# A one-core kernel of two graph layers: row products one unit later in layer 0, and two reload sequences of the second step reordered

## The chip, the cores and the metric

The kernel runs on one core of a Trainium2 chip. The metric is the device time of one execution in microseconds (us). The engines are named as the profile names them: PE (TensorE), DVE (VectorE), ACT (ScalarE), POOL (GpSimd) and SP (SyncE), which issues all DMAs of this kernel in one order.

## The reference

N = 4096 nodes, 256 features. Layer 0 is a dense graph attention layer with 4 heads, layer 1 a two-step diffusion with a learned sparse attention; each is followed by a residual and a layer norm.

```python
# layer 0
h = inputs @ W                                   # hr = h as (N, 64, 4)
e = s_src[:, None, :] + s_dst[None, :, :]        # N x N x 4
e = where(e >= 0, e, -0.2 * e)
att = softmax(e * adj[:, :, None], axis=1)
out = einsum('ijh,jfh->ihf', att, hr) + bias + inputs @ res_w + res_b
x = layernorm(x + out)
# layer 1
R = adj + eye; R = R / R.sum(-1)                 # N x N
for n in range(2):
    A = top_p_attention(Xa, W1, W2, W3)          # softmax(q k^T), nucleus 0.9, rows renormalised
    Xf = R @ Xf
    Xa = A @ Xa
    Z = Z + Xf @ U1[n].T + Xa @ U2[n].T
x = layernorm(x + layernorm(x + Z))
```

## The kernel before, in words

Rows are worked in 32 tiles of 128 (NT = 32). Every engine has its own program, written out by hand, and semaphores tie them together; no scheduler moves anything.

**Layer 0** has 128 units u, one for each tile t = u // 4 and head h = u % 4. DVE makes the masked scores of a unit in `masked(u)`: an addition (L1386), the leaky step (L1388), and the multiplication with the tile's adjacency rows and row maximum (L1390), which waits for the adjacency tile (semaphore `s_adj`). Its result goes through one small POOL instruction (L568), which raises `s_u`; ACT waits for that in `ex(u)` (the exponential, L1063). ACT then does `linear(u + 2)` (L1057), whose result DVE's L1388 of unit u + 2 waits for, and four copies of transposed chunks out of PSUM, `ev` (L1070). PE transposes the chunks (`turn`, L845) and multiplies them with the features (`pv`, L796). Once in a tile there are further pieces. In unit u % 4 = 0 ACT copies the tile's output (`out_turned`, L1104) and a transposed normalised tile (`ev_x`, L1080), and PE does `turn_back` (L804 to L809). In the next unit ACT copies the residual output (`ev_y0`, L1096). In unit u % 4 = 2 and 3 DVE does the layer norm (`post_a`, `post_b`).

The **row products** `rows(r)` on PE (L835, L828) multiply the normalised tile r of the layer's result with the two matrices U1 and the key and query matrix; `ev_rows(r)` on ACT (L1086, L1087) copies them out and raises `s_gx`. SP stores them: it waits for `s_gx`, issues three stores (`xf_d`, `gx_d`, `kq_d`), and then, in the next turn of its loop, loads the next adjacency tile (`in_adj`, 2 MB) into the one of two buffers that came free, stores the normalised tile (`X_d`) and loads a piece of xT:

```python
for t in range(NT + 3):
    if 1 <= t < NT:
        if t >= 2: sp.wait_ge(s_u, 4 * (t - 1))
        ld(adj_s[t % 2], tile_of(adj, t), s_adj[t % 2])
    ...
    if 2 <= t < NGX + 2:
        r = t - 2
        sp.wait_ge(s_gx, 2 * (r + 1))
        ...
```

**Layer 1** keeps the two operands `xa` and `xf` whole in SBUF (32 row tiles each). A step s does for each tile n the logits (`logits`, L927), the search of the nucleus threshold on DVE (L1477 to L1610) with help of POOL (`bracket`, L600 to L623) and ACT (`level`, L1235 and L1236), the transposes (`Tr`, L972), the product with `xa` (`AV`, L986), and the small products (`mq`, L950). In the second step (s = 1) PE also does `Rmul(r)` (L911), 32 matmuls (eight for each of four chunks) of a row tile of adj with `xf`, to which POOL adds the unit matrix's part: r = 0 to 31 is the first hop and r = 32 to 63 the second, whose operand is the first hop's result y. A row tile of R needs four chunks of 512 KB (`adjTb`), which go through three buffers; SP loads chunk q + 3 once PE is through with chunk q (semaphore `R`). PE does Rmul(0) and Rmul(1) ahead of the tile loop, then two of them in each tile, and `gather_level(n)` (L992) between, ahead of which DVE can't finish its tile (L1591 waits for it). POOL's `r_post` normalises a row tile of R's product, SP stores it (`rstore`: `y_d` for the first hop, `z_d` for the second). `xa` is loaded again ahead of the second step (`reload`, from `xa_d`), `xf` is loaded again from `y_d` ahead of Rmul(32) (`chunked(xf, y_d)`), eight loads of four row tiles each (semaphores `s_xl[0..7]`).

Of the kernel before, what the change touches and what calls it, by code (L numbers as in the profile page):

```python
# [26 lines left out]
def gat_topp_kernel(nc, xT, x, adj, adjTb, Wp, WT, aT, res_w, bias, res_b, ident, sel,  # L27
                    W1, W2T, W3T, U1T, U2T, ln_g, ln_b, out):
    N = adj.shape[0]
    NT = N // 128  # L30
    TBK = min(8, NT)
    NCH = NT // TBK
# [10 lines left out]
    AJR = 3  # L43
    XA = 257
    NQ = N // 512
    HT = NT // 2
    CT = 4
# [8 lines left out]
    def pairs_in(n):  # L56
        if n < 0:
            return [0]
        if n == 0:
            return list(range(1, RLEAD + 1))  # L60
        return [n + RLEAD] if n + RLEAD < NT else []

    ctx = ExitStack()
    with ctx:
# [21 lines left out]
        def sem(name):  # L86
            return ctx.enter_context(nc.semaphore(name))
# [30 lines left out]
        ys = cst.take(2, 256)  # L118
# [32 lines left out]
        xf = r1.take(NT, XA)  # L151
# [6 lines left out]
        u2 = r1.take(2, 256)  # L158
# [48 lines left out]
        y_d = nc.dram_tensor("y_d", [N, 256], F32).ap()  # L207
# [14 lines left out]
        def tile_of(d, t):  # L222
            return d[t * 128:(t + 1) * 128, :]
# [62 lines left out]
        s_l1 = sem("s_l1")  # L286
# [16 lines left out]
        gslot = {}  # L303
        i = 0
        for u in range(NU):
            if u % 4 == 1 and u >= 9:
                gslot[(u - 9) // 4] = i
                i += 1
            for c in range(NCH):
                slot_of[u * NCH + c] = i  # L310
                i += 1
            if u % 4 == 0 and u >= 8:
                xslot[(u - 8) // 4] = i
                i += 1
# [7 lines left out]
        st = []  # L322
        for s in range(2):
            g = {}
# [17 lines left out]
        def _(sp):  # L342
            def ld(dst, src, s):
                sp.dma_start(dst, src).then_inc(s, 16)
# [59 lines left out]
            qload(0, 0)  # L404
            qload(0, 1)

            def chunked(dst, src):
                for q in range(NQ):
                    ld(dst[:, CT * q:CT * (q + 1), 0:256],
                       src[CT * 128 * q:CT * 128 * (q + 1), :].rearrange("(t p) n -> p t n", p=128), s_xl[q])  # L410

            g = st[0]
# [8 lines left out]
            for q in range(AJR):  # L421
                t, c = divmod(q, NCH)
                ld(aj[:, q % AJR], adjTb[t][:, c * CW:(c + 1) * CW], st[1]["aj"][q % AJR])
            for q in range(NQ):
                hi = min(CT * (q + 1), NGX)
                ld(xf[:, CT * q:hi, 0:256],
                   xf_d[CT * 128 * q:128 * hi, :].rearrange("(t p) n -> p t n", p=128), s_xf)
            def reload(q):
                sp.wait_ge(g["av"], (NT - 1) * NCH + q // 2 + 1)
                sp.wait_ge(g["acc"], CT * (q + 1))  # L430
                for i in range(2):
                    sp.wait_ge(g["xd"][i], 16 * (CT // 2) * (q + 1))
                ld(xa[:, CT * q:CT * (q + 1), 0:256],
                   xa_d[CT * 128 * q:CT * 128 * (q + 1), :].rearrange("(t p) n -> p t n", p=128), s_xl[q])

# [26 lines left out]
                    sp.wait_ge(g["acc"], n - 2)  # L462
                    ld(tile_of(h_d, n - 3), hh, g["nz"])
            sp.wait_ge(g["gd"], 16 * (NT - NGX))
            for q in range(NQ):
                reload(q)
            sp.wait_ge(g["ks"], 16 * NT)
            sp.wait_ge(s_bar, 5 * kS[0])

            sp.wait_ge(g["nz"], 16 * NT)  # L470
            g = st[1]
            ld(u2, U2T[1].rearrange("(k p) n -> p k n", p=128), s_l1)

            def adjchunk(q):
                if q >= 2 * NT * NCH:
                    return
                if q >= AJR:
                    sp.wait_ge(g["R"], q - AJR + 1)
                t, c = divmod(q, NCH)
                ld(aj[:, q % AJR], adjTb[t % NT][:, c * CW:(c + 1) * CW], g["aj"][q % AJR])  # L480

            def gxload(p):
                if p < HT:
                    for i in range(2):
                        ld(gxi[:, i, :], tile_of(gx_d, 2 * p + i), g["gi"])

            def adjpairs(n, half):
                for p in pairs_in(n):
                    for q in range((2 * p + half) * NCH, (2 * p + half + 1) * NCH):
                        adjchunk(q + AJR)  # L490

            def rstore(n):
                for p in pairs_in(n):
                    for i in range(2):
                        r = 2 * p + i
                        sp.wait_ge(g["yd"], r + 1)
                        ld(tile_of(y_d if r < NT else z_d, r % NT), yr[:, i, :], g["ys"])
                    gxload(p + 1)

            gxload(0)  # L500
            adjpairs(-1, 0)
            sp.wait_ge(g["xp"], 1)
            qload(1, 2)
            adjpairs(-1, 1)
            for n in range(LAST + 4):
                if n + 3 < NT:
                    sp.wait_ge(g["xp"], n + 2)
                    qload(1, n + 3)
                if 3 <= n < NT + 2:
                    sp.wait_ge(g["acc"], n - 2)  # L510
                    ld(tile_of(h_d, n - 3), hh, g["nz"])
                if 2 <= n < NT + 2:
                    ld(hin, tile_of(h_d, n - 2), g["hi"])
                if n - 3 in fslot:
                    m = fslot[n - 3]
                    for r in (2 * m, 2 * m + 1):
                        if r < DR:
                            sp.wait_ge(g["fo"], r + 1)
                        else:
                            sp.wait_ge(g["lo"], r - DR + 1)  # L520
                        ld(tile_of(out, r), fin[:, r % 6, :], g["fd"])
                if n in fslot:
                    m = fslot[n]
                    if m >= 3:
                        sp.wait_ge(g["fd"], 32 * (m - 2))
                    if m == HT - 1:
                        sp.wait_ge(g["lz"], 2)
                    elif m >= 1:
                        sp.wait_ge(g["fa"], 2 * m)
                    if m >= 2:  # L530
                        sp.wait_ge(g["f1"], 2 * (m - 1))
                    sp.wait_ge(g["nz"], 16 * min(2 * m + 2, NT - 1))
                    sp.wait_ge(g["ys"], 16 * (NT + 2 * m + 2))
                    for i in range(2):
                        r = 2 * m + i
                        if r < NT - 1:
                            ld(fin[:, r % 6, :], tile_of(h_d, r), g["fi"])
                        ld(finz[:, i, :], tile_of(z_d, r), g["fi"])
                        ld(finx[:, r % 4, :], tile_of(X_d, r), g["fi"])
                if HT in pairs_in(n):  # L540
                    rstore(n - 1)
                    sp.wait_ge(g["ys"], 16 * NT)
                    sp.wait_ge(g["R"], NT * NCH)
                    chunked(xf, y_d)
                adjpairs(n, 0)
                if HT not in pairs_in(n):
                    rstore(n - 1)
                adjpairs(n, 1)
# [181 lines left out]
        def _(pe):  # L730
# [100 lines left out]
            def rows(t):  # L831
                pe.wait_ge(s_ev, xslot[t] + 1)
                b = slot0(gslot[t])
                for k in range(2):
                    mm(b[:, 0:512], xts[:, k, :], u10[:, k, :], start=(k == 0), stop=(k == 1))  # L835
                keys(t, b[:, 512:640]).then_inc(s_t, 1)
# [12 lines left out]
            pe.wait_ge(s_gu, 16 * 2)  # L849
            for u in range(NU):  # L850
                g0 = u * NCH
                if u % 4 == 1 and u >= 9:
                    rows((u - 9) // 4)
                if u >= 1:
                    pv(g0 - 2)
                    pv(g0 - 1)
                for c in range(NCH):
                    turn(g0 + c)
                if u % 4 == 0 and u >= 8:
                    turn_x((u - 8) // 4)  # L860
                pv(g0)
                pv(g0 + 1)
                if u >= 4 and u % 4 == 0:
                    turn_back(u // 4 - 1)
# [15 lines left out]
            for s in range(2):  # L880
                g = st[s]
# [146 lines left out]
        def _(ac):  # L1028
# [53 lines left out]
            def ev_rows(t):  # L1082
                i = gslot[t]
                ac.wait_ge(s_t, i + 1)
                ac.wait_ge(s_of, t + 2)
                act(ots, bank(2 * (i % 3)), ACT.Copy).then_inc(s_gx, 1)  # L1086
                act(xts[:, 0, :], bank(2 * (i % 3), 2)[:, 512:640], ACT.Copy).then_inc(s_gx, 1)  # L1087
                ac.wait_ge(s_gx, 2 * (t + 1))
                ac.sem_inc(s_ev, 1)
# [36 lines left out]
            for u in range(NU):  # L1126
                if u >= 2:
                    ex(u)
                if u % 4 == 1 and u >= 5:
                    ev_y0(u // 4 - 1)  # L1130
                if 3 <= u + 2 < NU:
                    linear(u + 2)
                if u % 4 == 1 and u >= 9:
                    ev_rows((u - 9) // 4)
                for c in range(NCH):
                    ev(u * NCH + c)
                    if c == 1 and u >= 4 and u % 4 == 0:
                        out_turned(u // 4 - 1)
                if u % 4 == 0 and u >= 8:
                    ev_x((u - 8) // 4)  # L1140
# [17 lines left out]
            for s in range(2):  # L1158
                g = st[s]
# [136 lines left out]
                for n in range(NT + 2):  # L1296
# [5 lines left out]
                    if 1 <= n <= NT:  # L1302
                        for c in range(NCH):
                            q = (n - 1) * NCH + c
# [431 lines left out]
```

## Time and profile before

| | |
|---|---|
| median of 3 runs | 3900.14 us (3897.62 to 3902.06) |
| time of the profiled execution | 3899.62 us |
| its span, first to last instruction | 3897.8 us |
| layer 0 | 0 to about 1412 us |
| first step of layer 1 | about 1412 to 2201 us |
| second step | about 2201 us to the end |
| PE, DVE, ACT, POOL busy | 3592.3, 3558.7, 3059.3, 1524.9 us |
| granted clock, mean | 0.985 |

The busy shares are means over stages whose limits differ, so each stage is to be read by itself; an engine's idle time costs something only where the others wait for it.

### The profile page before, as it was taken

What the parts mean: (1) busy time and instruction counts of PE and PEld (TensorE: products, weight loads), DVE (VectorE), ACT (ScalarE), POOL (GpSimd) and SP (SyncE); (2) the same over time, 40 slices, a digit from 0 to 9 for tenths busy, and PEclk for the clock granted to TensorE, in tenths of its full rate; (3) what the DMA queues carried; (4) which work ended last, traced back from release to release, by engine and by line L of the source; (5) the groups of instructions that cost most, each with busy time, mean ns of one, the idle gap of its engine ahead of it and who ended that gap; (6) DMA issues with size and microseconds to landing.
All of it is one profiled execution on the core that took longest, in us unless ns stands there. A gap on an engine that the chain in (4) does not pass through costs nothing.

```text
span 3897.8 us, 66233 instructions
## 1 busy us (share of the span) xinstructions
PE 3592.3 (92%) x25368; PEld 3026.4 (78%) x25368; DVE 3558.7 (91%) x6048; ACT 3059.3 (78%) x3107; POOL 1524.9 (39%) x1627
## 2 busy tenths in 40 slices
PE   8888888888888859999999989999999999999996
PEld 5777777777777747778777768888888788888885
DVE  4999999999999969999999499999999899999998
ACT  6999999999999955555555378888888788888873
POOL 0112112112112101111111155556555469999997
PEclk9999999999999979999999989999999999999998
DMA  2112112112112140000000323333333433333332
GB/s 109 52 57 84 57 57 84 57 57 84 57 57 84 57 135 15 17 17 17 20 19 19 106 87 94 99 99 99 105 105 104 130 109 112 113 115 115 116 119 69
DMA packets 155583, 302.72 MB, mean 78 GB/s; under 512 B 16635, under 2 KB 116987, under 8 KB 151011
## 3 DMA queue, kind: packets, MB, share of 16 engines
q1 hardware_dynamic: 155234, 298.22, 23.7%
q8 instruction: 201, 3.29, 0.3%
q14 instruction: 148, 1.20, 0.1%
HBM read 256.54 MB, written 41.62 MB: 76 GB/s over the span
## 4 chain that ended last, share of the span: by engine, by line
ACT 36%; POOL 22%; DVE 17%; PE 15%; issue 10%; DMA 1%; DVEq 0%; ACTq 0%; SPq 0%; POOLq 0%; PEldq 0%; PEld 0%
ACT b L1070 8%; ACT b L1063 7%; ACT b L1235 6%; ACT b L1236 6%; DVE b L1440 5%; DVE b L1610 3%; PE ps L796 3%; ACT b L1057 3%; DVE b L1498 3%; DVE b L1496 2%; POOL b L608 2%; POOL b L605 2%; ACT b L1216 2%; PE ps L986 2%; PE ps L845 2%
## 5 line engine op out<-in xcount | busy, mean ns | idle before, releaser
L911 PE MATMUL ps<-b 128*128 128x257 f32 x4096 | 912.8, 382 | 20.4 <-DMA b<-in_adjTb 11.0
L986 PE MATMUL ps<-b 128*128 128x257 f32 x4096 | 902.8, 380 | 0.0
L911 PEld LDWEIGHTS ps<-b 128*128 128x128 f32 x4096 | 777.7, 191 | 146.4 <-DMA b<-in_adjTb 12.3
L986 PEld LDWEIGHTS ps<-b 128*128 128x128 f32 x4096 | 771.9, 190 | 113.2 <-issue 0.8
L845 PE MATMUL ps<-cb,b 128*128 128x128 f32 x4096 | 498.4, 277 | 188.0 <-ACT b L1063 147.2
L845 PEld LDWEIGHTS ps<-cb,b 128*128 128x128 f32 x4096 | 446.6, 142 | 238.4 <-ACT b L1063 170.1
L1388 DVE SCALAR_TENSOR_TENSOR b<-b 128x4096 f32<-128x4096 f32 x128 | 566.4, 4425 | 17.4 <-ACT b L1057 13.8
L1390 DVE CUSTOM_DVE_ANT_0 b<-b 128x4096 f32<-128x4096 f32 x128 | 566.4, 4425 | 4.4
L1070 ACT ACTIVATE b<-ps 128x1024 f32<-128x1024 f32 x512 | 494.6, 1079 | 48.5 <-PE ps L845 48.5
L568 POOL TENSOR_SCALAR b<-b 128x1 f32<-128x1 f32 x128 | 75.3, 588 | 1087.9 <-DVE b L1390 1087.9
L1063 ACT ACTIVATE b<-b 128x4096 f32<-128x4096 f32 x128 | 485.3, 3791 | 0.0
L796 PE MATMUL ps<-b 128*64 128x128 f32 x8192 | 482.3, 275 | 0.0
L796 PEld LDWEIGHTS ps<-b 128*64 128x64 f32 x8192 | 443.9, 137 | 24.9 <-issue 10.8
L1477 DVE SCALAR_TENSOR_TENSOR b<-b 128x4096 f32<-128x4096 f32 x99 | 446.7, 4512 | 3.5
L1235 ACT ACTIVATE b<-b 128x4096 fp8e4<-128x4096 f32 x93 | 345.0, 3709 | 7.9 <-ACT b L1187 5.7
L1236 ACT ACTIVATE b<-b 128x4096 fp8e4<-128x4096 f32 x93 | 344.9, 3709 | 3.0
L1610 DVE SCALAR_TENSOR_TENSOR b<-b 128x4096 f32<-128x4096 f32 (+1 forms) x67 | 287.4, 4293 | 43.3 <-issue 28.9
L1057 ACT ACTIVATE b<-b 128x2560 f32<-128x2560 f32 x128 | 321.5, 2512 | 0.0
L1307 ACT ACTIVATE b<-ps 128x1024 f32<-128x1024 f32 x256 | 242.2, 1031 | 45.9 <-PE ps L972 45.7
L972 PE MATMUL ps<-cb,b 128*128 128x128 f32 x2048 | 241.9, 278 | 34.7 <-DVE b L1610 33.4
L972 PEld LDWEIGHTS ps<-cb,b 128*128 128x128 f32 x2048 | 231.5, 143 | 46.4 <-DVE b L1610 42.0
L1216 ACT ACTIVATE b<-b 128x4096 f32<-128x4096 f32 x64 | 237.0, 3703 | 24.4 <-DVE b L1426 19.2
(205 smaller groups left out, 5050.2 us busy)
## 6 DMA issues: line engine op xcount, KB each, us to landing
b<-in_adjTb SPq DMA_DIRECT2D x256, 512.0 KB, 3.7
b<-in_adj SPq DMA_DIRECT2D x32, 2048.0 KB, 8.6
h_d<-b SPq DMA_DIRECT2D x63, 128.0 KB, 1.8
b<-h_d SPq DMA_DIRECT2D x63, 128.0 KB, 2.5
b<-in_xT SPq DMA_DIRECT2D x4, 1024.0 KB, 8.6
b<-in_xT SPq DMA_DIRECT2D x32, 128.0 KB, 8.4
gx_d<-b SPq DMA_DIRECT2D x32, 128.0 KB, 1.8
X_d<-b SPq DMA_DIRECT2D x32, 128.0 KB, 8.5
```

The lines of the kernel that those rows point to most:

```text
L796: last = mm(bank(6 + t % 2)[half, 128 * h:128 * h + 128], h_s[:, j, 64 * h:64 * h + 64], pt[:, gq % PTR, b, :], start=(j < 2), stop=(j >= ...
L845: last = nc.tensor.transpose(o[:, b * 128:(b + 1) * 128], ub[:, u % UB, j * 128:(j + 1) * 128], ident_s)
L911: last = mm(b[:, 0:XA], aj[:, q % AJR, e, :], xf[:, j, :], start=(j == 0), stop=(j == NT - 1))
L972: last = nc.tensor.transpose(o[:, b * 128:(b + 1) * 128], scores(s, t)[:, j * 128:(j + 1) * 128], ident_s)
L986: last = mm(o[:, 0:XA], at[:, q % ATR, b, :], xa[:, j, :], start=(j == 0), stop=(j == NT - 1))
L1063: act(b, b, ACT.Exp, bias=nm[:, u % 4:u % 4 + 1], accum_out=zp[:, u % 16:u % 16 + 1]).then_inc(s_x, 1)
L1070: act(pt[:, gq % PTR].rearrange("p a b -> p (a b)"), bank(2 * (i % 3), 2)[:, 0:CW], ACT.Copy).then_inc(s_ev, 1)
L1235: alink(act(junk, e, ACT.Sign, bias=neg, accum_out=C, saturate=False))
L1236: alink(act(junk, e, ACT.Relu, bias=neg, accum_out=S, saturate=False))
L1388: link(v.scalar_tensor_tensor(out=b, in0=b, scalar=SLOPE, in1=b, op0=ALU.mult, op1=ALU.max))
L1390: v.tensor_tensor_reduce(out=b, in0=b, in1=adj_s[t % 2], scale=1.0, scalar=-3.0e38, op0=ALU.mult, op1=ALU.max, accum_out=nm[:, u % 4:u % 4 ...
L1477: link(v.scalar_tensor_tensor(out=VN, in0=E, scalar=mid, in1=E, op0=ALU.is_gt, op1=ALU.mult, accum_out=G))
```

## The change

Three places change. `rows` and `ev_rows` move by one unit on PE and ACT, from u % 4 = 1 (u from 9) to u % 4 = 2 (u from 10). At the start of the second step SP issues adjacency chunks 3 to 6 of R among the eight reloads of `xa`, one chunk ahead of each two reloads, and the load of `u2` goes behind them. Ahead of Rmul(32), seven of the eight reloads of `xf` are issued as soon as row tiles 0 to 29 of y are stored, and only the eighth waits for the last two (30 and 31).

```diff
-            if u % 4 == 1 and u >= 9:
-                gslot[(u - 9) // 4] = i
+            if u % 4 == 2 and u >= 10:
+                gslot[(u - 10) // 4] = i
...
-            def chunked(dst, src):
-                for q in range(NQ):
+            def chunked(dst, src, lo=0, hi=NQ):
+                for q in range(lo, hi):
...
             sp.wait_ge(g["gd"], 16 * (NT - NGX))
-            for q in range(NQ):
-                reload(q)
             sp.wait_ge(g["ks"], 16 * NT)
             sp.wait_ge(s_bar, 5 * kS[0])
             sp.wait_ge(g["nz"], 16 * NT)
             g = st[1]
-            ld(u2, U2T[1].rearrange("(k p) n -> p k n", p=128), s_l1)
...
+            for c in range(NCH):
+                adjchunk(AJR + c)
+                for q in range(NQ // NCH * c, NQ // NCH * (c + 1)):
+                    reload(q)
             gxload(0)
-            adjpairs(-1, 0)
+            ld(u2, U2T[1].rearrange("(k p) n -> p k n", p=128), s_l1)
             sp.wait_ge(g["xp"], 1)
...
                 if HT in pairs_in(n):
+                    sp.wait_ge(g["ys"], 16 * (NT - 2))
+                    sp.wait_ge(g["R"], NT * NCH)
+                    chunked(xf, y_d, 0, NQ - 1)
                     rstore(n - 1)
                     sp.wait_ge(g["ys"], 16 * NT)
-                    sp.wait_ge(g["R"], NT * NCH)
-                    chunked(xf, y_d)
+                    chunked(xf, y_d, NQ - 1, NQ)
...
-                if u % 4 == 1 and u >= 9:
-                    rows((u - 9) // 4)
+                if u % 4 == 2 and u >= 10:
+                    rows((u - 10) // 4)
...
-                if u % 4 == 1 and u >= 9:
-                    ev_rows((u - 9) // 4)
+                if u % 4 == 2 and u >= 10:
+                    ev_rows((u - 10) // 4)
```

On ACT, around the first row product of layer 0 (units 9 and 10), the order before is this; L1063 is `ex`, L1057 `linear`, L1070 `ev`, L1096 `ev_y0`, L1086 and L1087 `ev_rows`:

```order
L1063 ACTIVATE b<-b 128x4096
L1096 ACTIVATE b<-ps 128x256
L1057 ACTIVATE b<-b 128x2560
L1086 ACTIVATE b<-ps 128x512
L1087 ACTIVATE b<-ps 128x128
L1070 ACTIVATE b<-ps 128x1024 x4
L1063 ACTIVATE b<-b 128x4096
L1057 ACTIVATE b<-b 128x2560
L1070 ACTIVATE b<-ps 128x1024 x4
```

In the change the same place reads as follows; every line number of this part of the file is 3 higher.

```order
L1066 ACTIVATE b<-b 128x4096
L1099 ACTIVATE b<-ps 128x256
L1060 ACTIVATE b<-b 128x2560
L1073 ACTIVATE b<-ps 128x1024 x4
L1066 ACTIVATE b<-b 128x4096
L1060 ACTIVATE b<-b 128x2560
L1089 ACTIVATE b<-ps 128x512
L1090 ACTIVATE b<-ps 128x128
L1073 ACTIVATE b<-ps 128x1024 x4
```

The two copies now stand behind the exponential and the linear step of the next unit. SP's own order in layer 0 is the same, and it waits for these copies ahead of its three stores and of the adjacency load behind them.

SP's issues at the start of the second step move as follows.

```order
 L344 DMA h_d<-b 128x256
-L344 DMA b<-xa_d 128x4x256 x8
+L344 DMA b<-in_adjTb 128x1024
+L344 DMA b<-xa_d 128x4x256 x2
+L344 DMA b<-in_adjTb 128x1024
+L344 DMA b<-xa_d 128x4x256 x2
```

Chunk 3 of R now stands ahead of all reloads, where it stood behind the eight of them, but it waits for PE to be through with chunk 0, and the reloads now wait behind it.

At the second hop of R (tile 15 of the second step) SP's order before, with the semaphores it waits for, is the following.

```order
L344 DMA h_d<-b 128x256 [waits acc_1]
L344 DMA b<-h_d 128x256
L344 DMA y_d<-b 128x256 [waits yd_1] x2
L344 DMA b<-y_d 128x4x256 [waits R_1,ys_1]
L344 DMA b<-y_d 128x4x256 x7
L344 DMA b<-in_adjTb 128x1024 [waits R_1] x8
```

In the change it is this.

```order
L344 DMA h_d<-b 128x256 [waits acc_1]
L344 DMA b<-h_d 128x256
L344 DMA b<-y_d 128x4x256 [waits R_1,ys_1]
L344 DMA b<-y_d 128x4x256 x6
L344 DMA y_d<-b 128x256 [waits yd_1] x2
L344 DMA b<-y_d 128x4x256 [waits ys_1]
L344 DMA b<-in_adjTb 128x1024 [waits R_1] x8
```

Seven of the reloads have come ahead of the two stores that wait for POOL.

## Rows read from the trace of the kernel before

**Rows 1.** Windows of layer 0 and of the second step: length, busy time of each engine

```profile
600.00:1000.00 400.00, 343.23 (x3988) 307.49 (x3984) 393.02 (x208) 388.01 (x316) 73.61 (x56) 1.00 0.18 62
2600.00:2800.00 200.00, 200.00 (x983) 166.72 (x982) 184.98 (x328) 166.51 (x184) 116.71 (x116) 1.00 0.33 101
```

**Rows 2.** Timeline of ACT, one tile of layer 0: start, length, line [idle before]

```profile
903.24 3.79 ACT L1063 ACTIVATE b<-b 128x4096 f32<-128x4096 f32 x1
...
913.61 3.84 ACT L1063 ACTIVATE b<-b 128x4096 f32<-128x4096 f32 x1
...
919.88 0.73 ACT L1086 ACTIVATE b<-ps 128x512 f32<-128x512 f32 x1
...
922.12 3.77 ACT L1070 ACTIVATE b<-ps 128x1024 f32<-128x1024 f32 x4 [1.34 <-PE ps L845]
925.75 3.73 ACT L1063 ACTIVATE b<-b 128x4096 f32<-128x4096 f32 x1
...
931.78 3.77 ACT L1070 ACTIVATE b<-ps 128x1024 f32<-128x1024 f32 x4
...
945.02 3.79 ACT L1063 ACTIVATE b<-b 128x4096 f32<-128x4096 f32 x1
```

**Rows 3.** Timeline of DVE, same tile, unit u % 4 = 0 and the next

```profile
932.00 4.43 DVE L1388 SCALAR_TENSOR_TENSOR b<-b 128x4096 f32<-128x4096 f32 x1 [0.27 <-ACT b L1057]
936.46 4.43 DVE L1390 CUSTOM_DVE_ANT_0 b<-b 128x4096 f32<-128x4096 f32 x1
...
940.81 1.02 DVE L1386 TENSOR_SCALAR b<-b 128x1536 f32<-128x1536 f32 x1
```

**Rows 4.** Timeline of POOL behind that unit

```profile
940.98 0.92 POOL L568 TENSOR_SCALAR b<-b 128x1 f32<-128x1 f32 x1 [10.09 <-DVE b L1390]
```

**Rows 5.** Timeline of SP's queue, same tile

```profile
920.81 0.32 SPq L344 DMA_DIRECT2D xf_d<-b  x1
...
922.14 0.44 SPq L344 DMA_DIRECT2D b<-in_adj  x1
```

**Rows 6.** Waits of SP's queue: total, times, longest

```profile
SPq L344 <- ACT b L1087: 1166.4, 30, 43.2
```

**Rows 7.** DMAs that read in_adj, all 32: issue to landing

```profile
DMA to landing us min/median/max: 7.6/8.6/15.4
```

**Rows 8.** Timeline of ACT, unit 5, which has turn_back ahead but no row products

```profile
121.85 3.84 ACT L1063 ACTIVATE b<-b 128x4096 f32<-128x4096 f32 x1
...
131.74 3.89 ACT L1063 ACTIVATE b<-b 128x4096 f32<-128x4096 f32 x1
```

**Rows 9.** Timeline of PE, start of the second step

```profile
2220.64 6.80 PE L911 MATMUL ps<-b 128*128 128x257 f32 x16 [4.91 <-DMA b<-in_adjTb]
...
2279.49 6.39 PE L911 MATMUL ps<-b 128*128 128x257 f32 x16 [6.13 <-DMA b<-in_adjTb]
```

**Rows 10.** Chain that ended last, same stretch: start, length, work

```profile
2272.59 0.74 POOL b L657
...
2274.68 4.77 DMA b<-in_adjTb
```

**Rows 11.** Timeline of PE: starts of Rmul(30), Rmul(32) and Rmul(34)

```profile
2978.17 14.07 PE L911 MATMUL ps<-b 128*128 128x257 f32 x64
...
3038.28 16.59 PE L911 MATMUL ps<-b 128*128 128x257 f32 x64 [9.34 <-ACTq L1259]
...
3091.41 14.07 PE L911 MATMUL ps<-b 128*128 128x257 f32 x64
```

**Rows 12.** Timeline of SP's queue ahead of Rmul(32)

```profile
3030.03 2.94 SPq L344 DMA_DIRECT2D y_d<-b  x2
3034.36 6.91 SPq L344 DMA_DIRECT2D b<-y_d  x8
```

**Rows 13.** Waits of DVE between 3040 and 3100 us

```profile
DVE b L1591 <- PE ps L992: 14.1, 1, 14.1
```

**Rows 14.** Timeline of ACT, copy of the AV product one tile earlier

```profile
2986.83 0.38 ACT L1257 ACTIVATE b<-ps 128x257 f32<-128x257 f32 x1
```

More of the change, by code:

```diff
@@ L428, in reload @@
             def reload(q):
-                sp.wait_ge(g["av"], (NT - 1) * NCH + q // 2 + 1)
-                sp.wait_ge(g["acc"], CT * (q + 1))
+                sp.wait_ge(st[0]["av"], (NT - 1) * NCH + q // 2 + 1)
+                sp.wait_ge(st[0]["acc"], CT * (q + 1))
                 for i in range(2):
-                    sp.wait_ge(g["xd"][i], 16 * (CT // 2) * (q + 1))
+                    sp.wait_ge(st[0]["xd"][i], 16 * (CT // 2) * (q + 1))
                 ld(xa[:, CT * q:CT * (q + 1), 0:256],
```

## The prediction

> **What bounds the kernel now.** I read the windows first, since three stages are changed and each has its own limit. In layer 0, DVE is busy 393 of 400 us and ACT 388, while PE has room; in the middle of the second step PE is busy in all of 200 us [rows 1]. So layer 0 has to be read on ACT and DVE, the second step on PE.
>
> In layer 0 one tile of four units repeats every 945.02 - 903.24 = 41.78 us [rows 2]. In it ACT waits once, 1.34 us, for PE: the copies of unit u % 4 = 1 come late, because PE has `turn_back` and the row products ahead of that unit's transposes. DVE waits once too, 0.27 us, for ACT's linear step [rows 3]. Nothing else in the tile waits, so DVE's own work takes 41.78 - 0.27 = 41.51 us a tile, and that is the floor of layer 0.
>
> SP's queue is the third thing to look at, because a row product's copies release it. SP waits for the second of the two copies (L1087) 30 times, 1166.4 us in all [rows 6], far more than for anything else in this layer. Behind this wait stand the three stores and then the next adjacency tile: copies begin at 919.88, the first store is issued at 920.81, the adjacency load at 922.14 [rows 2, 5]. A load lands 7.6 us after its issue at best and 8.6 us in the median [rows 7], so this one is there at 922.14 + 8.6 = 930.7. DVE needs it at 936.46, when the masked multiplication of the next tile's first unit starts [rows 3]. It has 5.7 us to spare.
>
> **Layer 0, part by part.** The change takes 1.34 us of wait from ACT (PE starts the transposes of unit 1 earlier by the length of the row products) and moves the two copies behind the next exponential and linear step. That puts `s_gx`, and with it the adjacency load, later by 12.14 us (913.61 to 925.75) less the 1.34 us and less the copies' own 0.90 us (919.88 to 920.78, which is 922.12 less the wait) = 9.90 us. This is the time of an unhindered unit with `ev_y0`: unit 5, which has `turn_back` ahead of it but no row products, takes 131.74 - 121.85 = 9.89 us [rows 8], so PE without the row products is indeed in time. 9.90 is more than the 5.7 us to spare. DVE would wait 4.2 us in the first tiles, and behind L1390 stand all the rest of its queue and, through `s_u`, ACT's exponentials.
>
> The stall doesn't stay at 4.2 us, because DVE is several units' steps ahead of ACT, and the stall eats this lead until ACT waits for DVE. Then the times go round in a loop, which I add up link by link:
>
> - from the start of L1390 with the adjacency tile to the end of POOL's step, 941.90 - 936.46 = 5.44 us [rows 3, 4]; POOL's instruction takes 0.92 us, as it ends with DVE's next instruction, L1386, and that one follows in the change as well;
> - from the exponential of unit 0 to that of unit 1, 913.61 - 903.24 = 10.37 us [rows 2];
> - from that of unit 1 to that of unit 2, 9.90 us, as above;
> - from there to where the copies now stand, 931.78 - 925.75 = 6.03 us [rows 2];
> - the copies until SP's first store, 920.81 - 919.88 = 0.93 us, and the three stores until the load's issue, 922.14 - 920.81 = 1.33 us [rows 2, 5];
> - the load's landing, 8.6 us [rows 7].
>
> The sum is 5.44 + 10.37 + 9.90 + 6.03 + 0.93 + 1.33 + 8.6 = 42.60 us. It is longer than DVE's 41.51 us, so the loop decides, and DVE waits 42.60 - 41.51 = 1.1 us in each tile. Against 41.78 us of before, each tile takes 0.82 us more. The wait on `s_gx` stands ahead of the loads of adjacency tiles 3 to 31, that is 29 landings with 28 whole loops between: 28 x 0.82 = **+23.0 us**. Entering the loop and leaving it I set at zero; each may be 1 us either way. The landing is the loosest link. With the fastest landing, 7.6 us, the loop is 41.6 us and layer 0 gains 28 x 0.18 = 5 us; with 9.1 us, half a microsecond above the median, it is 43.1 us and costs 37 us. A median over 28 loads moves far less than a single one, so I take 8.6 with 8.3 to 8.9 around it, +15 to +31 us.
>
> On this link the Trainium skill speaks against my sum: "DMA: Bandwidth & Descriptors", section "Anatomy of one DMA", fits a DMA of that path as 2.0 us plus the bytes over 436 GB/s, for 2 MB an estimate of 6.8 us. The loop would then be 40.8 us, shorter than DVE's work, and there would be no stall. No load of this trace was that fast, and three stores are issued ahead of this one; the measured landing is what I use, and the page's case is the second rival.
>
> **Start of the second step.** PE waits 4.91 us for chunk 3 of R, which stands behind eight reloads in the queue, and 6.13 us for chunk 15 [rows 9]. The change takes the first wait away: chunk 3 is released when PE is through with chunk 0 and is alone in the queue. But the second one ends when POOL, at 2272.59 + 0.74 us, is through with the second row tile of the first hop, after which SP comes to chunk 15, which lands 4.77 us after 2274.68 [rows 10]. POOL's chain up to there comes from the threshold search of tiles 0 and 1, which needs the logits and none of the row products, so it doesn't move. PE arrives at chunk 15 earlier and waits for it longer: the gain is **0**. If the chain did follow PE, 4.91 us and the slower first matmuls after it would be at stake, 4.91 + 6.80 - 3.52 = 8.2 us (16 matmuls take 14.07 / 4 = 3.52 us when nothing slows them [rows 11]). I take 5 us as the likely size of that case, since DVE and POOL would then be the next to be waited for. The reloads of `xa` are now released by PE's chunks 0 to 3, all of which are done before 2220.64 + 6.80 = 2227.4. They are hidden: the product that reads them comes behind chunk 15 on PE, after 2279.49, and if they took those 50 us they would still be in time. The issues of the eight reloads delay chunks 4 to 6, which stand between them, by an issue or two each; what PE may lose by that before chunk 15 is covered by the same wait, 6.13 + 4.91 = 11 us of it.
>
> **The second hop of R.** PE's pairs of row products start 50.61 us apart when nothing is in the way; from Rmul(30) to Rmul(34), two such periods, the trace has 3091.41 - 2978.17 = 113.24 us [rows 11]. For the ordinary period I take (3091.41 - 3038.28) less the 16.59 - 14.07 = 2.52 us by which Rmul(32) ran long, 50.61 us. So 113.24 - 2 x 50.61 = 12.02 us are lost there: 9.34 us of wait, and the rest in the first matmuls after it. The reloads of `xf` are issued from 3034.36 on, once POOL and SP are through with y's last two tiles (3030.03) [rows 12], and PE starts 3.9 us later. In the change seven reloads are issued when the first hop is through on PE, 2978.17 + 2 x 14.07 = 3006.3, and SP has issued what stands ahead, about 3009 us: some 20 us ahead of PE's need at 3028.9 (3038.28 - 9.34). Only the eighth is issued at 3034.36, and PE needs it after 7/8 of Rmul(32), at 3028.9 + 12.3 = 3041.2; at 3.9 us of landing it is there at 3038.3. Chunk 131 of R goes out right behind it, at about 3035, and is needed after 3/4, at 3039.5. With 3.9 us of landing and some more behind the other, it may come 0.3 us late. DVE waited 14.1 us for PE here [rows 13], more than the 12 us, so it follows PE all the way, and PE bounds the rest. The gain is 12.0 - 0.3 = **11.7 us**, 8 at the least if chunk 131 is late by a few us and the clock falls again.
>
> **Sum.** The profiled execution took 3899.6 us (span 3897.8 and 1.8 around it), 0.5 less than the median of the runs. 3899.6 + 23.0 + 0 - 11.7 = 3910.9 us, in the runs' median some 3911.
>
> **Rivals.**
> 1. *The adjacency load still comes in time* (faster). If the loop is shorter than 41.51 us, that is, if loads land in under 7.5 us, DVE's own work bounds layer 0, the change gives 28 x 0.27 = 7.6 us there and 11.7 in the second hop: 3880 us. Against it stands the best landing of 7.6 us. Chance 0.12.
> 2. *The loop binds, but by less*: a landing near 8.1 us, or POOL's step at a third of its 0.92 us. Loop 42.0 to 42.2 us, +6 to +12 us, 3894 to 3900 us in all. Chance 0.13.
> 3. *The second hop gives nothing.* The wait row names ACT's L1259 as releaser, the mark that the AV product was copied. One tile earlier Rmul(30) starts at 2978.17 and that copy comes at 2986.83 [rows 11, 14], so PE does not need it; it had come by chance when the reload landed. If it were the cause all the same, 3922 us. Chance 0.08.
> 4. *The start of the second step pays as well*, up to 5 us: 3906 us. Chance 0.12.
>
> My forecast keeps 0.55. The range of 8 in 10 goes from 3893 us (rival 2's lower half and all of rival 1 left out) to 3922 us. The forecast's own is 3903 to 3919. About 0.2% (7.8 us) is what a measurement of this kernel can tell from no change. Slower by more than that are most of the forecast, rival 3 and a third of rival 4: 0.60. Within it are the rest of rival 4, rival 2 and the forecast's lower edge: 0.27. Faster is rival 1: 0.13.
>
> **What would show it.** In layer 0: a tile's period near 42.6 us, DVE's L1390 waiting about 1.1 us a tile for `in_adj`, no wait of ACT for L845, and ACT's exponential waiting for POOL. At the start of the second step: no wait of 4.9 us, one of 11 us at chunk 15, and L992 no earlier against the step's start. At Rmul(32): no wait over 1 us. I am wrong if the period of layer 0 is below 41.78 us, or if PE still waits 9 us ahead of Rmul(32).

## The result, and the profile after

The changed kernel takes 3941.36 us in the median of four runs (3938.39 to 3945.07); the kernel before, run beside it, 3900.44. The ratio is 1.0106, with a 95% interval of 1.0089 to 1.0124: slower by 41 us, where I had forecast 11 us with a range up to 3922. The profiled execution took 3941.5 us, with a span of 3939.7.

The page of the changed kernel says where to look. These are its span and two of its costliest groups of instructions (busy time in us and mean length in ns, then the idle time of the engine just before them and what ended it). Before, the page named nobody for whom DVE's multiplication with the adjacency tile or ACT's exponential waited.

```profile
span 3939.7 us, 66234 instructions
...
L1393 DVE CUSTOM_DVE_ANT_0 b<-b 128x4096 f32<-128x4096 f32 x128 | 566.4, 4425 | 67.9 <-DMA b<-in_adj 64.5
...
L1066 ACT ACTIVATE b<-b 128x4096 f32<-128x4096 f32 x128 | 479.1, 3743 | 56.7 <-POOL b L571 56.7
```

DVE now waits 64.5 us for the adjacency loads (L1393 is L1390 of before, L1066 is L1063), in 29 waits, and ACT waits behind it, through POOL's L571. This is the loop of the prediction. Its links in one tile (tile 19), on ACT:

```profile
895.05 3.71 ACT L1066 ACTIVATE b<-b 128x4096 f32<-128x4096 f32 x1 [2.52 <-POOL b L571]
...
902.62 1.03 ACT L1073 ACTIVATE b<-ps 128x1024 f32<-128x1024 f32 x1 [0.54 <-PE ps L848]
...
906.30 3.72 ACT L1066 ACTIVATE b<-b 128x4096 f32<-128x4096 f32 x1
...
910.42 0.39 ACT L1099 ACTIVATE b<-ps 128x256 f32<-128x256 f32 x1 [0.31 <-PE ps L812]
...
916.97 3.74 ACT L1066 ACTIVATE b<-b 128x4096 f32<-128x4096 f32 x1
...
922.99 0.61 ACT L1089 ACTIVATE b<-ps 128x512 f32<-128x512 f32 x1
```

And on SP, DVE and ACT, where the loop closes:

```profile
923.79 0.32 SPq L344 DMA_DIRECT2D xf_d<-b  x1
...
925.12 0.45 SPq L344 DMA_DIRECT2D b<-in_adj  x1
...
934.09 4.43 DVE L1393 CUSTOM_DVE_ANT_0 b<-b 128x4096 f32<-128x4096 f32 x1 [2.99 <-DMA b<-in_adj]
...
939.55 3.71 ACT L1066 ACTIVATE b<-b 128x4096 f32<-128x4096 f32 x1 [2.18 <-POOL b L571]
```

Read against [rows 2 to 5]: from the issue to DVE's start 8.97 us, from there to the exponential of unit 0 5.46 us, from the copies to the load's issue 2.13 us, all near what was forecast. But from the exponential of unit 0 to that of unit 1 the tile takes 11.25 us instead of 10.37, and from there to unit 2 10.67 us instead of 9.90. In both ACT waits for PE. PE's rows and the clock that it was granted tell why. The first fence is the timeline of PE. The second has windows: the two stretches around the first of these rows, and 400 us of layer 0. Each row gives the length, the busy time of PE, of its weight loads, of DVE, ACT and POOL, then the granted clock as a share of full speed, and last the DMA's share and rate.

```profile
898.91 6.13 PE L848 MATMUL ps<-cb,b 128*128 128x128 f32 x32 [4.33 <-ACT b L1066]
...
931.45 2.84 PE L848 MATMUL ps<-cb,b 128*128 128x128 f32 x24 [1.69 <-ACT b L1066]
```

```profile
895.00:898.90 3.90, 0.00 (x0) 0.00 (x0) 3.90 (x1) 3.85 (x3) 0.02 (x1) 0.77 0.00 0
898.90:903.00 4.10, 4.09 (x19) 4.09 (x20) 4.07 (x2) 3.56 (x3) 0.00 (x0) 0.50 0.00 0
...
600.00:1000.00 400.00, 346.50 (x3790) 312.34 (x3790) 371.49 (x199) 371.77 (x301) 71.78 (x54) 0.94 0.18 62
```

The stall leaves PE idle for 4.33 us ahead of unit 0's transposes, where it was idle for 1.69 us before; the granted clock then is 0.50, the lower of its two levels (1.2 GHz), and 32 transposes take 6.13 us where they take 3.71 at full clock. The second row of PE is the last unit of the same tile: 1.69 us of idle time, and transposes at full speed. From 600 to 1000 us the clock is 0.94 in the mean, where it was 1.00 [rows 1].

The loads of tiles 3 and 31 are issued at 179.27 and 1403.05 us:

```profile
179.27 0.44 SPq L344 DMA_DIRECT2D b<-in_adj  x1
...
1403.05 1.66 SPq L344 DMA_DIRECT2D b<-in_adj  x1
```

That is (1403.05 - 179.27) / 28 = 43.71 us a tile against 41.78 before, 28 x 1.93 = 54 us. The second step makes good a part of this. PE's timeline in it:

```profile
2255.46 3.70 PE L930 MATMUL ps<-kr 64*128 64x512 f32 x16 [1.35 <-ACTq L233]
...
2287.77 3.75 PE L914 MATMUL ps<-b 128*128 128x257 f32 x16 [0.23 <-DMA b<-in_adjTb]
...
2299.54 2.08 PE L930 MATMUL ps<-kr 64*128 64x512 f32 x4 [5.25 <-ACT b L1176]
...
2333.32 5.79 PE L914 MATMUL ps<-b 128*128 128x257 f32 x16 [6.28 <-DMA b<-in_adjTb]
...
3092.51 3.75 PE L914 MATMUL ps<-b 128*128 128x257 f32 x16 [0.20 <-DMA b<-in_adjTb]
...
3132.79 14.07 PE L914 MATMUL ps<-b 128*128 128x257 f32 x64
```

The wait for chunk 3 is gone (the 0.23 us are chunk 7's), another (5.25 us, in the logits) has come, and the one for chunk 15, 6.28 us, is as long as it was, 6.13 [rows 9]; 11 us had been forecast. Rmul(32) waits 0.20 us for its last chunk and for nothing ahead of it, where it waited 9.34 us [rows 11]; Rmul(34) starts 3132.79 - 2255.46 = 877.33 us after the step's first logits. Before, those started at 2201.39, 890.02 us ahead of [rows 11]'s 3091.41. So the second step is 12.7 us shorter, and it starts 2255.46 - 2201.39 = 54.1 us later.

### The profile page after: what moved, and what is told of

Read it like the earlier page. It is cut to its first block, busy times and chain, and to the rows that moved or that the text cites. A ratio compares the mean times of both kernels' runs of the same rounds, so it can differ in the third digit from the quotient of the medians.

```text
span 3939.7 us, 66234 instructions
## 1 busy us (share of the span) xinstructions
PE 3641.5 (92%) x25368; PEld 3073.2 (78%) x25368; DVE 3558.7 (90%) x6048; ACT 3074.5 (78%) x3107; POOL 1522.7 (39%) x1627
## 4 chain that ended last, share of the span: by engine, by line
PE 34%; ACT 23%; DVE 18%; issue 10%; POOL 7%; DMA 7%; SPq 1%; DVEq 0%; ACTq 0%; POOLq 0%; PEldq 0%; PEld 0%
PE ps L914 11%; PE ps L989 7%; DMA b<-in_adj 6%; PE ps L848 5%; DVE b L1443 4%; ACT b L1238 4%; ACT b L1239 4%; ACT b L1066 4%; DVE b L1613 3%; ACT b L1073 3%; PE ps L799 3%; DVE b L1501 3%; DVE b L1499 2%; ACT b L1060 2%; PE ps L975 2%
## 5 line engine op out<-in xcount | busy, mean ns | idle before, releaser
L848 PE MATMUL ps<-cb,b 128*128 128x128 f32 x4096 | 545.1, 293 | 191.1 <-ACT b L1066 169.1
L848 PEld LDWEIGHTS ps<-cb,b 128*128 128x128 f32 x4096 | 494.5, 152 | 238.4 <-ACT b L1066 184.8
L1393 DVE CUSTOM_DVE_ANT_0 b<-b 128x4096 f32<-128x4096 f32 x128 | 566.4, 4425 | 67.9 <-DMA b<-in_adj 64.5
L1391 DVE SCALAR_TENSOR_TENSOR b<-b 128x4096 f32<-128x4096 f32 x128 | 566.4, 4425 | 12.7 <-ACT b L1060 8.5
L1066 ACT ACTIVATE b<-b 128x4096 f32<-128x4096 f32 x128 | 479.1, 3743 | 56.7 <-POOL b L571 56.7
L571 POOL TENSOR_SCALAR b<-b 128x1 f32<-128x1 f32 x128 | 75.3, 588 | 1146.1 <-DVE b L1393 1146.1
L1060 ACT ACTIVATE b<-b 128x2560 f32<-128x2560 f32 x128 | 314.6, 2458 | 0.0
L975 PE MATMUL ps<-cb,b 128*128 128x128 f32 x2048 | 241.2, 277 | 34.4 <-DVE b L1613 33.0
L975 PEld LDWEIGHTS ps<-cb,b 128*128 128x128 f32 x2048 | 230.5, 143 | 46.3 <-DVE b L1613 41.8
L930 PE MATMUL ps<-kr 64*128 64x512 f32 x1024 | 242.1, 612 | 20.6 <-ACT b L1176 11.7
```

The costliest lines, as they stand in the source:

```text
L848: last = nc.tensor.transpose(o[:, b * 128:(b + 1) * 128], ub[:, u % UB, j * 128:(j + 1) * 128], ident_s)
L975: last = nc.tensor.transpose(o[:, b * 128:(b + 1) * 128], scores(s, t)[:, j * 128:(j + 1) * 128], ident_s)
L1066: act(b, b, ACT.Exp, bias=nm[:, u % 4:u % 4 + 1], accum_out=zp[:, u % 16:u % 16 + 1]).then_inc(s_x, 1)
L1391: link(v.scalar_tensor_tensor(out=b, in0=b, scalar=SLOPE, in1=b, op0=ALU.mult, op1=ALU.max))
L1393: v.tensor_tensor_reduce(out=b, in0=b, in1=adj_s[t % 2], scale=1.0, scalar=-3.0e38, op0=ALU.mult, op1=ALU.max, accum_out=nm[:, u % 4:u % 4 ...
```

## The experiments

The table gives all ten, in medians of their runs; the ratio is to the kernel before, run beside each. That kernel's own median moved from 3897.9 to 3900.4 us between these sessions, so a difference of two medians from two sessions is uncertain by some 2.5 us.

| kernel | us | ratio (95%) |
|---|---|---|
| the change | 3941.4 | 1.0106 (1.0089 to 1.0124) |
| e1 row products back at u % 4 = 1 | 3887.1 | 0.9967 (0.9955 to 0.9979) |
| e2 row products moved alone | 3958.8 | 1.0148 (1.0126 to 1.0170) |
| e3 early reload of xf alone | 3887.7 | 0.9968 (0.9956 to 0.9980) |
| e4 adjacency load ahead of the wait | 3880.1 | 0.9949 (0.9935 to 0.9962) |
| e5 the same, row products back | 3887.7 | 0.9973 (0.9963 to 0.9983) |
| e6 load ahead of the three stores | 3910.4 | 1.0031 (1.0018 to 1.0044) |
| e7 32 fill matmuls | 3986.0 | 1.0227 (1.0211 to 1.0243) |
| e8 row products at u % 4 = 3 | 4243.0 | 1.0885 (1.0865 to 1.0905) |
| e9 16 fill matmuls | 3916.0 | 1.0043 (1.0026 to 1.0060) |
| e10 e9 and e6 together | 3898.5 | 0.9999 (0.9990 to 1.0009) |

**e1: the row products go back.** In the changed kernel, in the slot order, on PE and on ACT:

```diff
-            if u % 4 == 2 and u >= 10:
-                gslot[(u - 10) // 4] = i
+            if u % 4 == 1 and u >= 9:
+                gslot[(u - 9) // 4] = i
```

> The change with the row products of layer 0 put back to u % 4 = 1; the two reload parts stay. Theory L (the adjacency load, released by the row products' copies, closes a loop that sets layer 0): layer 0 is that of before, 41.78 us a tile and no wait of DVE for in_adj, so only the gains of the second step are left: PE's Rmul(34) comes 11.9 us earlier against the step's start plus 0.8 us at the step's beginning, 3900 - 12.7 = 3887.5 us. Rival R (the two reload parts cost something in the queue that the row products' wait hid): above 3890 us.

Measured 3887.1 us, against an expected 3887.5. DVE waits for no adjacency load, and its 0.3 us waits for L1060 are back. So no loss is left without the move of the row products.

**e2: the move alone.** The same edit the other way round, in the kernel before.

> The kernel before with the row products alone moved to u % 4 = 2. Theory L: the whole loss of layer 0 and nothing else, 3900 + 54 = 3954 us, mean tile 43.7 us, DVE waiting some 64 us for in_adj in 29 waits. Rival: the parts work upon one another, and the sum of e1 and e2 (-12.7 + 54 = +41) is missed by over 5 us.

Measured 3958.8 us; its runs spread from 3944.8 to 3966.4, and the profiled one took 3954.7. The sum of e1 and e2 is -13.3 + 58.4 = +45 us in the medians, against +41 for the change; with e2's profiled execution (3954.7) in place of its median it is +41. The parts add up within e2's spread of 22 us, and no closer than that is shown. DVE waits 66.6 us for `in_adj`, in 29 waits.

**e3: the early reload of xf alone.** The last part of the change's diff, in the kernel before.

> The kernel before with the early reload of xf from y alone (seven of eight reloads ahead of the last two stores). Theory: the wait of 9.3 us ahead of Rmul(32) and the slow matmuls behind it go, 3900 - 11.9 = 3888.5 us, and the first part of the reload change, e1 less e3, is worth 1 us or less. Rival (PE waits there for ACT's copy of the AV product): no change, 3900 us.

Measured 3887.7 us. In the waits of PE around Rmul(32) only this is left:

```profile
PE ps L913 <- DMA b<-in_adjTb: 0.2, 1, 0.2
```

The wait for ACT that the row of before named is gone with the order of the reload, while ACT's work is untouched: the reload had been the cause. e1, which has the reordered start of the step too, is 0.5 us faster, less than the runs can tell.

**e4: the load ahead of the wait.** SP issues adjacency tile t and only then waits for the row products' copies of tile t - 3 and stores them:

```diff
                     ld(adj_s[t % 2], tile_of(adj, t), s_adj[t % 2])
+                if 3 <= t < NGX + 3:
+                    r = t - 3
+                    sp.wait_ge(s_gx, 2 * (r + 1))
+                    ...
-                if 2 <= t < NGX + 2:
-                    r = t - 2
-                    sp.wait_ge(s_gx, 2 * (r + 1))
-                    ...
```

> The change, but SP issues each adjacency load of layer 0 ahead of its wait for the row products' copies (the three stores come behind the load). Nothing else moves. Theory L: the loop is open, DVE never waits for in_adj, ACT no longer waits 1.34 us for PE in unit 1, and DVE's own 41.51 us a tile is the floor: layer 0 is 7 us shorter than before, 3900 - 7.5 - 12.7 = 3880 us. Rival P (the place of the row products between the transposes of unit 1 and 2 makes PE or ACT late by itself, and the adjacency wait is only where it shows): a tile stays above 41.78 us, 3888 us or more.

Measured 3880.1 us, where 3880 was expected: 61 us faster than the change and 20 us faster than the kernel before. The timeline of SP has the issue of tile 4's load, and under it the view of the tile `in_adj` the first and the last issue of all 32 loads:

```profile
181.08 0.33 SPq L344 DMA_DIRECT2D b<-in_adj  x1
```

```profile
L344 SPq DMA_DIRECT2D b<-in_adj x32: 328/333/1257, 6.5 to 1302.8; - x32
```

(1302.8 - 181.08) / 27 = 41.54 us a tile: DVE's own work, 41.51 us by the forecast, is the floor. The view names nobody who waits for these loads any more.

**e5: is it the order or the move that wins in e4?** e4 with e1's edit.

> As e4 (adjacency load ahead of the wait for the row products), but with the row products back at u % 4 = 1. Theory: in that place the load was in time anyway, so the order of SP gives nothing, ACT waits its 1.34 us for PE again, a tile takes 41.78 us: 3887.5 us, as e1. Rival (what e4 won came from the earlier load, not from the move of the row products): 3880 us, as e4.

Measured 3887.7 us, as e1. With the load in time anyway SP's order gives nothing. The 7.6 us between e5 and e4 are the move of the row products, as forecast for the case that the load comes in time (28 x 0.27). These medians are from two sessions (by the ratios it is 10 us), but the timelines have the same size: the exponentials of units 12 and 127 lie 1201.35 us apart in e5 and 1194.10 in e4, 7.2 us less.

**e6: one link 1.33 us shorter.** The load is issued right behind the wait for the copies, and the three stores behind it:

```diff
                     sp.wait_ge(s_gx, 2 * (r + 1))
+                    if t + 1 < NT:
+                        sp.wait_ge(s_u, 4 * t)
+                        ld(adj_s[(t + 1) % 2], tile_of(adj, t + 1), s_adj[(t + 1) % 2])
                     ...
```

> The change, with the adjacency load issued right behind the wait for the row products' copies, ahead of the three stores instead of behind them: one link of the loop is 1.33 us shorter. Theory L with the clock (the stall makes PE idle, its next transposes run at half the clock, and that lengthens two further links): without the slow transposes the loop is 42.6 - 1.3 = 41.3 to 41.4 us, under DVE's 41.51, so the stall, PE's idle time and the slow transposes all go together, a tile takes 41.5 to 41.8 us, and the run 3880 to 3888 us, over 50 us less for 1.33 us a tile. Rival (each link counts by itself, and the slow transposes have nothing to do with the wait): 43.7 - 1.3 = 42.4 us a tile, 3904 us.

Measured 3910.4 us, which is neither. The loads are issued at 178.56 (tile 3) and 1372.64 (tile 31), 42.65 us a tile, 1.06 less than the change. The loop did not fall under DVE's floor, because another link took back half of the gain:

```profile
DMA to landing us min/median/max: 7.9/9.3/15.1
```

The loads land in 9.3 us in the median, not in 8.7 as in the change, with the stores now issued right behind them; from the issue to DVE's start it is 9.36 us in the mean instead of 8.73. My expectation had kept the landing as it was. The slow transposes are still there in 19 of 28 tiles. So this run tests neither side of its expectation; e9 does.

**e7 and e9: PE kept busy in the stall.** Fill matmuls, whose results are overwritten, are added ahead of PE's wait for unit 0's exponential. SP's order stays that of the change, so DVE still has to wait for the adjacency loads.

```diff
+                if c == 0 and u % 4 == 0 and u >= 12:
+                    fill = slot0(slot_of[gq])
+                    for _ in range(FILL):
+                        mm(fill[:, 0:128], ident_s, ident_s, start=True, stop=True)
                 if c == 0:
                     pe.wait_ge(s_x, u + 1)
```

> The change, with 32 matmuls of the identity with itself on PE in each unit u % 4 = 0 from unit 12 on, ahead of PE's wait for the exponential, into the PSUM slot that the transposes overwrite; the results are not used. PE is then busy for most of the 4 us in which it waits. Theory L with the clock: the transposes of that unit run at full clock (a row of 24 in 2.84 us instead of 32 in 5 to 6.6), the two links between the exponentials fall from 10.93 and 10.41 to 10.4 and 9.9 us, a tile takes 42.7 us, the run 3941 - 28 x 1.0 = 3913 us. Rival (PE is late by the order of its work and not by its clock): the extra matmuls give nothing or cost something, 3941 us or more.

With FILL = 32 it took 3986.0 us. This is on the rival's side, but it does not decide between the two, since the fill was too long: the 32 became 64 instructions of 7.41 us in all, which ended after the exponential, and PE itself came late in every tile. What can be read is the clock: the 32 transposes behind them took 3.66 us, though DVE waited 107.1 us for `in_adj`.

> As e7, with 16 fill matmuls instead of 32. In e7 they turned out as 64 instructions of 7.4 us in all, 3.4 us more than PE's wait, so that PE itself came late. 16 of them take 3.7 us of the 4.0 us. Theory L with the clock: the links between the exponentials are 10.4 and 9.9 us in every tile, the tile takes 8.7 + 5.46 + 10.4 + 9.9 + 6.02 + 2.2 = 42.7 us, the run 3941 - 28 x 1.0 = 3913 us. Rival (slow transposes aren't what made the links longer): 43.7 us a tile, 3941 us.

With FILL = 16, half of that, in the timeline of PE and under it in the windows:

```profile
917.11 3.84 PE L847 MATMUL ps<-cb 128*128 128x128 f32 x32
920.79 3.76 PE L853 MATMUL ps<-cb,b 128*128 128x128 f32 x32
```

```profile
600.00:1000.00 400.00, 374.74 (x4218) 335.58 (x4216) 385.54 (x205) 381.84 (x313) 74.81 (x56) 1.00 0.20 69
```

The fill takes 3.84 us, the transposes 3.76 us, and the clock from 600 to 1000 us is 1.00. Measured 3916.0 us, 25 us less than the change, for work that computes nothing. The loads of tiles 3 and 31 are issued at 179.98 and 1371.22 us, 42.54 us a tile; 42.60 was the forecast's loop. DVE still waits for `in_adj`, 32.4 us in 29 waits where it was 64.5, which is the 1.1 us a tile of the forecast. By the tiles e9 should be 28 x 1.17 = 33 us faster than the change; the profiled execution is 28.7 us faster. The other 4 us lie outside these tiles, and no run tells their cause.

**e8: one unit later still.**

```diff
-            if u % 4 == 2 and u >= 10:
+            if u % 4 == 3 and u >= 11:
```

> The change with the row products one unit later still, at u % 4 = 3. Theory L: the loop gets one unit of ACT longer, 9.6 us, so a tile takes 43.7 + 9.6 = 53.3 us or a little more, layer 0 28 x 11.5 = 323 us more than before, the run about 4210 us. Rival (the place at u % 4 = 2 is bad for its neighbours there, and the load is not what sets the tile): about that of the change or better, 3935 us.

Measured 4243.0 us, 33 more than expected. The loads of tiles 3 and 31 are issued at 192.09 and 1706.82 us, 54.10 us a tile, 0.8 more than expected (22 us of the 33); the load of tile 3 is issued 12.8 us later than in the change, and this entry into the loop stood in no sum. DVE waits 365.1 us for `in_adj`, and the clock of 600 to 1000 us is 0.88. Of the 10.39 us that a tile takes more than in the change, 9.66 are the unit of ACT that now stands ahead of the copies.

**e10: e9 and e6 together.**

> The 16 fill matmuls of e9 and the adjacency load ahead of the stores of e6 together. By the links measured in e6 (landing 9.36, 5.47, 6.02, 0.84) and full clock (10.4 and 9.9 us) the tile takes 42.0 us, 0.2 more than before: 3900 + 6 - 12.7 = 3893 us. Rival (the two don't add up): 3905 us or more.

Measured 3898.5 us, on the kernel before within 0.1%, 5 us above what the links gave. By the timeline rows of its tiles it is 9.53 us in the mean from the load's issue to DVE's start, not 9.36, and the tile takes 42.17 us, not 42.0, which is 28 x 0.17 = 5 us.

## Why the prediction was wrong

**What failed is one term, the +23.0 us of layer 0, which measured 54: two links of its loop were taken from a tile without the stall, with PE put down as having room.** The loop, its place, the count of waits (29) and the order of the links were right; that the stall would slow PE, and PE the loop, was missing. The links, each as the mean over tiles 3 to 30, read from the timeline rows of each tile:

| link | forecast | the change | e9 |
|---|---|---|---|
| issue of the load to L1390's start | 8.6 | 8.73 | 8.58 |
| to the exponential of unit 0 | 5.44 | 5.46 | 5.47 |
| to that of unit 1 | 10.37 | 10.93 | 10.39 |
| to that of unit 2 | 9.90 | 10.41 | 9.90 |
| to the row products' copies | 6.03 | 6.02 | 6.01 |
| to the next load's issue | 2.26 | 2.15 | 2.20 |
| sum | 42.60 | 43.71 | 42.54 |

Of the 1.11 us that the tile takes more than forecast, 0.56 and 0.51 are in two links. The failed step reads, in the prediction, "from the exponential of unit 0 to that of unit 1, 913.61 - 903.24 = 10.37 us" and "from that of unit 1 to that of unit 2, 9.90 us, as above". Both come from a tile in which PE never waits more than 1.69 us. The stall that I had worked out lies ahead of PE as well: PE idles 3.1 to 4.7 us, in 23 of the 28 tiles its clock is then at the lower level for all or part of the transposes, and for those there is no room. They delay ACT's copies of unit 0, `turn_back` behind them delays ACT's L1099 and unit 1's transposes, and ACT waits for PE, 0.54 + 0.31 + 0.21 us in the tile shown. (Its two links are 1.65 us longer than forecast; the rest of this stands in no wait of that size.) e9 is the test: PE kept busy in the same stall, both links fall to 10.39 and 9.90 us in every tile, and the tile to 42.54. In the change itself, the five tiles whose transposes ran at full clock have both links at 10.4 and 9.9 us too.

A longer link makes DVE's next wait longer: in the tiles behind those five it was 1.5 us in the mean, in the others 2.4. That PE's idle time grows with it is not shown, for it was 4.1 us behind those five and 3.7 in the others. I had seen the same effect in the second step ("the rest in the first matmuls after it") and counted it there, but not in the stall that I forecast myself. The Trainium skill has the rule in "TensorE: Matmul & The Clock Gate", section "Part 1: The HAM clock gate": the throttled clock is the state at rest, and activity releases it. The granted 0.50 behind PE's 4.33 us of idle time agrees.

**The landing**, to DVE's start, was 8.73 us where 8.6 was taken: 28 x 0.13 = 4 us of the 31, and the last link, 0.11 us shorter, gave 3 us back. Rival 1, which rests on a faster landing (3880 us), fell: the loads took 7.8 us at the least and 8.7 in the median. (The prediction calls it the second rival where it speaks of the page.) The 6.8 us worked out there come from a fit that "DMA: Bandwidth & Descriptors" of the Trainium skill, section "Anatomy of one DMA", gives for DMAs issued from GpSimd, while these loads are issued from SP; so the page did not speak against the sum, and the measured landing was the right one to use. What this rival says of the tile is right where the load is in time: e4, 3880.1 us.

**Rival 2** (the loop binds by less) fell with the same rows. **Rival 3** (the second hop gives nothing) fell by e3: the reload was the cause, and ACT's mark came by chance. The forecast gain was 11.7 us; from Tr(0), at 2349.41 in the change and at 2296.18 before, to Rmul(34) the step is (3091.41 - 2296.18) - (3132.79 - 2349.41) = 11.85 us shorter. Chunk 131 was 0.20 us late, 0.3 was forecast.

**Rival 4** (the start of the second step pays) was given up to 5 us, my sum 0, and 0 it is as far as the runs can tell. From the first logits to Tr(0) the change takes 93.95 us and the kernel before 94.79, but e2 and e3, which have the old order there, take 93.30 and 93.44, and e5, which has the new one, 94.74: the 0.84 us are scatter. The chain over POOL held, as forecast, but the wait did not go where I put it: of the 4.91 us won, PE lost 5.25 us again in a wait for ACT's L1176 that I had not foreseen, and the wait at chunk 15 did not grow.

**The sum**: the second step starts 54.1 us later and is 11.85 + 0.84 us shorter up to Rmul(34), +41.4 us; the medians differ by 41.

## What to carry to other kernels

When a step moves, look at which queue waits for it and what else stands behind that wait: here two small copies, moved by one unit, were in the way of a 2 MB load that has nothing to do with them, and issuing the load ahead of the wait (e4) turned 41 us of loss into 20 us of gain (12.7 of them the second step's). When a stall is forecast, the links of its loop may not be taken from rows without the stall; each engine that idles in it has to be asked what its next instructions cost, PE with its clock first. A releaser that a trace names is only the last one to report, and whether it was needed can be read from a neighbouring tile.

## What the runs showed of the hardware

- The length of an idle time near 3 to 4 us did not tell by itself what clock PE would have behind it. In one tile of the change 3.17 us of idle time were followed by transposes at half clock, in another 3.48 us by full clock:

```profile
502.01 6.60 PE L848 MATMUL ps<-cb,b 128*128 128x128 f32 x32 [3.17 <-ACT b L1066]
...
1291.42 2.84 PE L848 MATMUL ps<-cb,b 128*128 128x128 f32 x24 [3.48 <-ACT b L1066]
```

- In e4, 9 of the tiles 3 to 30 had slow transposes behind 2.4 to 2.6 us of idle time, and others full clock behind 2.6 us. The slow ones cost nothing there, since DVE was the bound: the tile took 41.54 us.
- 16 matmuls of 128 columns in f32 were 32 instructions of 3.84 us, and with them in each tile's stall the clock was 1.00 from 600 to 1000 us, where it was 0.94 without (e9 and the change).
- A 2 MB load landed later with three stores issued right behind it, 9.3 and 9.4 us in the median (e6, e10), than with them issued ahead of it, 8.7 and 8.5 us (the change, e9).
